# Three reorderings of the ScalarE and VectorE lists in a two-layer LoRA feed-forward kernel

## The reference

```
# layer 0: gated feed-forward (F = 1376) with three LoRAs of rank 16, then a sign-weight product
gate = x @ W_gate.T + 0.5 * (x @ A_gate[i].T) @ B_gate[i].T
up   = x @ W_up.T   + 0.5 * (x @ A_up[i].T)   @ B_up[i].T
act  = silu(gate) * up
down = act @ W_down.T + 0.5 * (act @ A_down[i].T) @ B_down[i].T
x    = x + down @ sign(weight).T + bias0
# layer 1: a LoRA of rank 16 by a second index, then a dense layer with 8 summed LoRAs
y    = (x @ B[j].T) @ A[j].T
x    = x + y @ W.T + (sum over 8 adapters of a scaled LoRA of y) + bias1
```

## Time and profile before

| | us |
|---|---|
| three runs | 994.11, 995.58, 997.29 (median 995.58) |
| the profiled execution: time | 994.71 |
| its span in the trace | 992.8 |

### The profile page before, as it was taken

How to read it: one execution, slowest core, us unless ns; L and a number is a source line. 1 busy time by engine, 2 the same in 40 slices (tenths; PEclk the granted TensorE clock), 3 DMA queues, 4 the chain that set the end, 5 groups by cost and what they waited for, 6 DMA issues and landing times.

```text
span 992.8 us, 19285 instructions
## 1 busy us (share of the span) xinstructions
PE 970.8 (98%) x5365; PEld 862.0 (87%) x5365; DVE 730.4 (74%) x1594; ACT 387.9 (39%) x669; POOL 386.5 (39%) x528
## 2 busy tenths in 40 slices
PE   8989989999999999999999999999999999999997
PEld 5878878998988889889989998899898888988896
DVE  5875777777777777777777777777777777778775
ACT  4753333334343333343433333344343333433332
POOL 0324333444444434444433434444433444343332
PEclk8999999999999999999999999999999999999999
DMA  9933434544444444444444544444445444434531
GB/s 352 360 90 105 108 98 125 141 111 120 125 117 111 127 133 136 110 119 129 116 109 127 138 120 121 115 131 112 118 128 140 118 123 115 128 101 127 132 103 43
DMA packets 155982, 128.64 MB, mean 130 GB/s; under 512 B 51648, under 2 KB 132800, under 8 KB 155840
## 3 DMA queue, kind: packets, MB, share of 16 engines
q1 hardware_dynamic: 145296, 94.37, 34.0%
q0 software_dynamic: 10672, 34.09, 12.2%
HBM read 86.45 MB, written 11.01 MB: 98 GB/s over the span
## 4 chain that ended last, share of the span: by engine, by line
SPq 38%; PE 26%; issue 12%; DVE 11%; DMA 10%; ACT 3%; DVEq 0%; ACTq 0%
SPq L344 16%; PE gu_ps L1038 14%; PE y_ps L1102 7%; DMA landed<-act_sb 6%; SPq L314 4%; SPq L322 4%; SPq L311 3%; SPq L319 3%; SPq L306 3%; DMA a_raw<-in_atab 3%; SPq L303 3%; PE y_ps L1038 3%; DVE act_sb L831 2%; DVE actT_sb L723 2%; PE out_ps L1038 1%
## 5 line engine op out<-in xcount | busy, mean ns | idle before, releaser
L1102 PE MATMUL y_ps<-down_sb,actT_sb 128*128 128x288 f32 x2112 | 297.0, 296 | 0.2
L1102 PEld LDWEIGHTS y_ps<-down_sb,actT_sb 128*128 128x128 f32 x2112 | 288.8, 189 | 6.6 <-issue 1.9
L1038 PE MATMUL gu_ps<-wg_sb,xT_sb 128*128 128x512 f32 (+1 forms) x1152 | 274.4, 387 | 0.0
L1038 PE MATMUL gu_ps<-wu_sb,xT_sb 128*128 128x512 f32 (+1 forms) x1152 | 260.4, 371 | 0.0
L1038 PEld LDWEIGHTS gu_ps<-wg_sb,xT_sb 128*128 128x128 f32 x1152 | 211.4, 188 | 35.9
L1038 PEld LDWEIGHTS gu_ps<-wu_sb,xT_sb 128*128 128x128 f32 x1152 | 206.9, 189 | 32.0
L723 DVE TENSOR_TENSOR b_sb<-b_raw,b_sb 64x1024 fp32r<-64x1024 f32 (+2 forms) x128 | 120.5, 941 | 72.1 <-ACT b_sb L499 57.7
L499 ACT CAST b_sb<-b_raw 64x1024 fp32r<-64x1024 f32 (+2 forms) x128 | 104.8, 819 | 100.7 <-DMA b_raw<-in_b1tab 99.9
L399 POOL DMA_INDIRECT b_raw<-in_btab,now x96 | 98.6, 1027 | 79.0 <-POOL now L413 75.1
L413 POOL TENSOR_TENSOR now<-now 128x1 int32<-128x1 int32 x160 | 50.1, 313 | 197.7 <-DVE b_sb L723 131.2
L499 ACT CAST actT_sb<-landed 128x512 fp32r<-128x512 f32 (+1 forms) x95 | 55.5, 584 | 168.2 <-DMA landed<-act_sb 155.4
(11 more groups left out here) (171 smaller groups left out, 953.0 us busy)
## 6 DMA issues: line engine op xcount, KB each, us to landing
landed<-act_sb SPq DMA_DIRECT2D x376, 64.0 KB, 2.1
ad_raw<-in_adtab SPq DMA_DIRECT2D x128, 88.0 KB
xT_raw<-in_xT SPq DMA_DIRECT2D x32, 256.0 KB
a_raw<-in_atab SPq DMA_DIRECT2D x128, 64.0 KB
x_sb<-in_x SPq DMA_DIRECT2D x31, 256.0 KB, 3.3
out_x<-x_sb SPq DMA_DIRECT2D x31, 256.0 KB
landed<-act_sb SPq DMA_DIRECT2D x128, 48.0 KB
b_raw<-in_b1tab SPq DMA_DIRECT2D x124, 32.0 KB
```

Source lines behind the costliest of these rows:

```text
L1038: last = nc.tensor.matmul(o, w, m, start=start and n == 0, stop=stop and n == len(terms) - 1, skip_group_check=not check)
L1102: last = nc.tensor.matmul(y_ps[half][:, 0:MH], actT_sb[:, ACTT_SLOT[c] + n, a, :], down_sb[:, blk, b, half * MH:(half + 1) * MH], start=c ...
```

## The change

Three things are moved. No instruction is added or removed, and TensorE's, SP's and POOL's lists stay as they are.

1. In every step with a `prev`, `split_td(prev)` comes first of the split operations that follow the landings on both engines. Before, ScalarE had it behind `split_actT(g, 0)` and `split_ad(g)`, and VectorE behind `split_actT(g, 0)`. Next comes `split_ad(g)`, then `split_actT(g, 0)`.
2. On ScalarE `silu(g, 2)` comes ahead of `split_actT(g, 1)`.
3. In step 0 t is masked, turned and split first on VectorE, ahead of the B rows of chunk 1, and on ScalarE right behind the copy of those rows. `split_up(2)`, which was ahead of step 0 on both engines, comes between the B rows of chunk 1 and those of chunk 2.

```diff
@@ ScalarE, step @@
                 split_b(g, 1)
                 if pp is not None:
                     split_x1(pp)
+                if prev is None:
+                    split_t(g)
+                    split_up(2, range(KC))
                 split_b(g, 2)
                 if pp is not None:
                     split_c(pp)
                 if prev is not None:
                     split_sbd(prev)
                     split_actT(prev, 2)
-                split_t(g)
+                    split_t(g)
...
                 if nxt is not None:
                     split_b(nxt, 0)
                     split_a(nxt)
+                if prev is not None:
+                    split_td(prev)
+                split_ad(g)
                 split_actT(g, 0)
-                split_ad(g)
-                if prev is not None:
-                    split_td(prev)
+                silu(g, 2)
                 split_actT(g, 1)
-                silu(g, 2)
                 if nxt is not None:
                     split_xT(nxt)
@@ ScalarE, ahead of step 0 @@
             rows_stored(act)
-            split_up(2, range(KC))
             step(0, None, None, 1)
@@ VectorE, step @@
                 if prev is not None:
                     gated(prev, 2)
                     turn_act(prev, 2)
+                if prev is None:
+                    own_t(g)
+                    turn_t(g)
+                    split_t(g)
                 split_b(g, 1)
+                if prev is None:
+                    split_up(2, range(KC))
                 if pp is not None:
                     split_x1(pp)
                 split_b(g, 2)
-                own_t(g)
-                turn_t(g)
+                if prev is not None:
+                    own_t(g)
+                    turn_t(g)
                 if pp is not None:
                     split_c(pp)
                     own_t1(pp)
-                split_t(g)
+                if prev is not None:
+                    split_t(g)
...
-                split_actT(g, 0)
                 if prev is not None:
                     split_td(prev)
                 split_ad(g)
+                split_actT(g, 0)
                 split_actT(g, 1)
```

## The result

The changed kernel takes 999.07 us in the median of 19 runs (996.06 to 1002.37), the kernel before 994.97 us in 19 runs beside them (993.40 to 998.18). The ratio is 1.0038, with a 95% interval of 1.0027 to 1.0049. The forecast was 987.0, in a range of 982 to 992.3, with 0.07 on slower. Both profiles show where it went. The profiled execution of the changed kernel was its slowest one (1002.37), so the sum of the stretches, 7.7 us, is larger than the 4.1 between the medians. In the stretches the sign is what counts.

What follows compares the result with a forecast made beforehand. It took a loop through SP, two landings, ScalarE and VectorE, slower than TensorE's step, as the bound. Gains of 3.7 (step 0), 2.4 (steps 1 to 3) and 2.5 us (steps 4 to 31) took 995.58 to 987.0, range 982 to 992.3.

Steps and rivals of the forecast that it cites:

- The two loops: Beside TensorE's 28.16 us a step runs a longer loop through SP, two landings, ScalarE and VectorE, 28.53 us a round.
- all waits are gain: Rival: TensorE is the bound and all its waits come back, 6.2 + 14.4 us, giving 975; chance 0.10.
- the last part: Expected profile: no td waits, `x1_done` waits of 0.2 to 0.5 us in most steps, `turn_x1` every 28.3 to 28.5 us.
- Steps 4 to 31: td split first in the loop: td waits vanish, rounds of 28.44 us, 2.5 us gained, bounds 0 to 6.2.
- Order on ScalarE: ScalarE's new order in the loop: cover of 0.2 to 0.4 us before chunk 1 lands, cost counted as 0.
- the slower rival: ScalarE's silu(g, 2) ahead of chunk 1's copy lengthens the loop; at 0.5 us a step 1001.5 us; chance 0.08.
- Step 0: t first: its wait and low clock go, gate(1, 0) comes 4.1 us earlier; 3.7 us counted, bounds 2.6 to 4.5.
- Steps 1 to 3: Step 2's td wait of 3.02 us and the low clock after it go; 2.4 us gained, bounds 0.7 to 4.
- only step 0 pays: Rival: the loop keeps 28.53 us a round, waits only move to `x1_done`, 992 us; chance 0.12.
- gather collisions: Rival: POOL's gathers collide with chunk 1's sends in the loop, 1.7 us each, four giving 993; chance 0.08.

Runs made afterwards that it cites:

- the short add: GpSimd adds only 8 of the 512 columns of bias0 in groups 0 to 30: changed kernel 989.32 us, kernel before 988.53 us.
- experiment 3: The changed kernel with silu(g, 2) back behind split_actT(g, 1) on ScalarE: 999.00 us, ratio 1.0059.
- experiment 8: The changed kernel with ScalarE's copy of ad moved ahead of its copy of td, VectorE's list kept: 991.33 beside 994.49 us, ratio 0.9979.
- experiment 11: The kernel before, with GpSimd's add of bias0 also waiting for VectorE's split of chunk 0: 997.92 us, ratio 1.0040.
- experiment 1: The kernel before with only the step 0 part of the change, loop order kept: 993.78 beside 994.24 us, ratio 1.0002.

## Why the prediction was wrong

- **The two loops: right, and it is what makes the rest readable.** TensorE's 28.16 us a step was not the bound. With all td waits gone the time did not fall, so the rival "all waits are gain" falls. The rule that the prediction set beside it, to optimize the engines on the critical path that TensorE idles for (Perfetto Trace Analysis of the Trainium skill, Optimization Strategies), would have picked the wrong engines by these waits. Those 13.2 us were TensorE waiting for the slower loop, and the waits moved to `x1_done` as the last part said.
- **Steps 4 to 31, the failed step.** It counted 2.5 us of gain, with a lower bound of 0; it was a loss of 9.6 in the profile. It took a duration for a property of the instruction: "there VectorE has chunk 0, td and ad (0.56, 0.2 and 0.8 us) still to do". In the very step it was read from, step 26, the trace of before has this:

```profile
824.26 1.27 POOL L434 TENSOR_TENSOR x_sb<-x_sb,bias_sb 128x512 f32<-128x512 f32 x1 [3.92 <-DMA x_sb<-in_x]
824.28 1.67 DVE L723 TENSOR_TENSOR actT_sb<-landed,actT_sb 128x384 fp32r<-128x384 f32 x1 [0.74 <-ACT actT_sb L499]
...
825.88 0.28 DVE L723 TENSOR_TENSOR tdT_sb<-tdT_raw,tdT_sb 128x128 fp32r<-128x128 f32 x1
```

  Chunk 0's split takes 1.67, not 0.56. In steps 7, 11, 15, 26 and 28 chunk 0's copy is late, but what made VectorE late for chunk 1 was this one split standing under GpSimd's add: with the short add leg 5 is 2.14 in every round of before, these steps included. The right reading was that before kept chunk 0's split clear of the add in 27 of 32 steps because it came right behind td's turn, and that the change puts two splits (td 0.29, ad 0.89 us) and two waits for ScalarE's copies (0.36 and 0.39) ahead of it. The range of this term had nothing for that.
- **"Order on ScalarE ... I count 0".** For silu and chunk 1's copy that held (experiment 3). What the part passed over is ScalarE's idle time ahead of td. By the medians ad's copy began 0.95 us ahead of the end of td's turn before, and begins 0.24 behind it after (2.34 ahead in experiment 8); chunk 0's copy went from 1.37 ahead to 0.92 behind. VectorE's split of ad stands 0.39 us for the copy. The part said "The split of chunk 0 itself ends near 24.2 ...: hidden", from TensorE's need of it. Its other cost, as the thing in front of chunk 1 on VectorE, wasn't looked at. No rival named this mechanism: the slower rival had the right sign and the wrong place.
- **Step 0, a term mis-sized.** 3.7 counted. The t wait and its low clock are gone as said (1.00 from 70 to 73), and VectorE turns chunk 1 at 77.73 in the profile, 3.3 us earlier after gate(0, 0) than before (3.6 forecast). But its landing takes longer, and TensorE, which arrives early, stands and falls to the low clock there:

```profile
77.02 0.71 DVE L772 STREAM_TRANSPOSE act_sb<-act_sb 128x512 f32<-128x512 f32 x1
...
78.39 0.90 POOL L399 DMA_INDIRECT b_raw<-in_btab,now  x1 [0.79 <-POOL now L413]
...
83.30 0.62 ACT L499 CAST actT_sb<-landed 128x512 fp32r<-128x512 f32 x1 [3.68 <-DMA landed<-act_sb]
...
85.84 4.50 PEld L1047 LDWEIGHTS gu_ps<-wg_sb,xT_sb 128*128 128x128 f32 x12 [3.67 <-POOL xT_sb L442]
```

  From the turn's end to the copy are 83.30 - 77.73 = 5.6 us, where "4.0 us" was carried over from before. In the kernel before the gather ahead of these sends was issued at 77.45, 2.5 us before the first of them; now it is at 78.39, between them. In the eight profiles with the new step 0 this stretch takes 4.8 to 5.6 us, in the five with the old one 4.0 to 4.2. That the gather is the cause is likely and not shown. I had that mechanism as a rival for the loop and not in this sum. The twelve weight loads take 4.50 us instead of the 2.46 of the earlier trace rows, at a granted clock of 0.50 from 85 to 90 (the level of 1.2 GHz), so 2.0 us of the clock's gain were lost again. Gate(1, 0) comes 2.3 us earlier, not 4.1.
- **Steps 1 to 3.** 2.4 counted. From gate(1, 0) to gate(3, 0) it is 58.80 us after and 60.26 before, 1.5 less. That is within its bounds, but not more than that: the stretch takes 56.3 to 60.3 us over all profiles, and 57.2 in experiment 11, whose order is that of before. And the earlier trace rows was read without the add. td's split of that step stood under it too (0.29 alone):

```profile
138.67 1.31 POOL L434 TENSOR_TENSOR x_sb<-x_sb,bias_sb 128x512 f32<-128x512 f32 x1 [4.33 <-DMA x_sb<-in_x]
...
139.18 0.95 DVE L723 TENSOR_TENSOR tdT_sb<-tdT_raw,tdT_sb 128x128 fp32r<-128x128 f32 x1 [0.32 <-ACT tdT_sb L499]
```

- **The range** ended at 992.3 because "nothing" was the worst case of the loop's term. A queue moved onto another one's cover had to have a bound below zero.
- **Two slips in the rivals**, neither of which moves the forecast. Step 0 as counted and the lower bound of steps 1 to 3 are 3.7 + 0.7 = 4.4 us, not 3.4, so "only step 0 pays" is 991.2. Four gather collisions at 1.7 us are 6.8 of the 8.6, far more than half: 993.8. The 1.7 itself stands on no row; the nearest is the 1.6 us of the landing in step 0.

**Still open.** Why step 0's 2.8 us don't show in the time of experiment 1: its rounds are 28.58 against 28.53, which gives 1.2 us back, within the scatter of profiles. What makes steps 1 to 3 differ by up to 4 us between profiles. And 0.13 us a round of the loss in the changed kernel's profile stand in legs 1 and 4, where no cause was shown.

## What to carry to other kernels

Before an instruction is moved on VectorE, look at what GpSimd does at its new place, and at the spread of its duration by form: two values for one shape (here 0.56 and 1.65 us) can be a collision and not work. A wait that is moved to the front of an engine's list must have ahead of it whatever that engine could do while it waits. And a wait of the busiest engine told only that something was late; the leg that closes the slower loop told what.

## What the runs showed of the hardware

A VectorE `tensor_tensor` with both inputs in SBUF made no progress while GpSimd's add of two SBUF operands ran. In the thirteen profiles of this case 391 splits, on five shapes, are long by more than 0.25 us under one of the two bias adds. Each ends at the same distance behind the add's end, to 0.01 us, wherever it began: 0.15 us for td (0.29 alone), 0.41 for chunk 0 (0.56), 0.55 for chunk 1 and the turned x1 (0.69), 0.75 for ad (0.88), 1.08 for the B rows (1.22). That is its own duration less 0.14. In step 26 above: 824.26 + 1.27 = 825.53, and 824.28 + 1.67 = 825.95, 0.42 later. The only other long ones, 13 pieces of the up weight, stand under GpSimd's subtraction (L442). 32x32 turns, which have one input, don't show it: 50 of td's turns lie under such an add and take 0.20 to 0.21 us, as elsewhere.

The other way round the add waits for the split. Its row grows from 1.29 to as much as 2.05 us (bias0) and 2.38 (bias1) when it comes up during a split, and in 280 of 281 such cases it ends 1.12 to 1.16 us behind that split's end. In experiment 8: 564.13 + 0.88 = 565.01, and 564.51 + 1.65 = 566.16.

The page SBUF — State Buffer of the Trainium skill states this in Who interferes with whom: a VectorE instruction with two SBUF inputs contends with a GpSimd instruction that reads SBUF, by an exclusive lock, and the order of issue decides which one blocks. The runs agree, with the numbers above. The prediction did not weigh it.
